# A four-layer graph network on one core: degrees counted by node tiles beside layer 0's messages, and inverse degrees found by a PE product inside layer 0

## The reference, cut to what matters

```python
x = layernorm(x + x @ W0)                  # W0: 256x256, edge weights scattered by (src, dst)
cnt = zeros((nodes, 4)).at[dst, etype].add(1.0)
inv_deg = 1.0 / maximum(cnt[dst, etype], 1.0)        # one number per edge
X = x
for l in range(4):
    h = einsum('ni,rio->rno', X, W[l])
    msg = h[etype, src] * inv_deg[:, None]
    agg = segment_sum(msg, dst)
    out = agg + X @ root[l] + bias[l]
    X = elu(layernorm(out) * gamma[l] + beta[l]) + X
out = layernorm(x + X)
```

## Time and profile before

| | |
|---|---|
| median of 3 runs | 2629.09 us (2626.32 to 2634.03) |
| the profiled execution's own time | 2628.71 us |
| its span | 2626.9 us |
| busy: PE, DVE, ACT, POOL | 82%, 55%, 11%, 59% |
| mean granted TensorE clock | 0.805 |

### The profile page before, as it was taken

How to read it: one execution, slowest core, us unless ns; L and a number is a source line. 1 busy time by engine, 2 the same in 40 slices (tenths; PEclk the granted TensorE clock), 3 DMA queues, 4 the chain that set the end, 5 groups by cost and what they waited for, 6 DMA issues and landing times.

```text
span 2626.9 us, 43114 instructions
## 1 busy us (share of the span) xinstructions
PE 2162.1 (82%) x7317; PEld 1284.5 (49%) x7320; DVE 1449.0 (55%) x4907; ACT 276.9 (11%) x538; POOL 1544.4 (59%) x1630
## 2 busy tenths in 40 slices
PE   4489667788888898888888989888889798887775
PEld 2254456664445554344455553445555444445554
DVE  6560999973445664234455652344556423456677
ACT  1114003310001111000011110000111100000000
POOL 3200600037777773777777737777777377777773
PEclk8589559996789998567889995678999956667778
DMA  5013300013444443334444433344444433334342
GB/s 165 0 41 144 130 8 0 0 42 106 120 129 138 145 149 96 105 105 121 129 136 146 145 104 104 106 120 129 138 145 147 140 110 104 105 104 121 105 121 64
DMA packets 103215, 280.43 MB, mean 107 GB/s; under 512 B 27676, under 2 KB 39050, under 8 KB 102798
## 3 DMA queue, kind: packets, MB, share of 16 engines
q0 software_dynamic: 75264, 205.62, 27.5%
q10 hardware_dynamic: 18224, 62.59, 6.2%
q1 hardware_dynamic: 9566, 10.42, 1.3%
HBM read 219.61 MB, written 58.91 MB: 106 GB/s over the span
## 4 chain that ended last, share of the span: by engine, by line
PE 50%; issue 13%; POOL 12%; DVE 9%; DMA 9%; DVEq 2%; POOLq 1%; ACT 1%; SPq 0%; ACTq 0%
PE acc L544 27%; POOL ring L335 12%; DMA ring<-h_rows,idx 8%; PE hp L463 8%; PE pw L463 7%; PE acc L533 3%; DVE S L993 3%; PE acc L536 2%; DVE hot_n L966 1%; DVE hot_s L966 1%; POOLq L204 1%; PE tr L452 1%; ACT XT L580 1%; DVEq L993 1%; PE pw L439 1%
## 5 line engine op out<-in xcount | busy, mean ns | idle before, releaser
L335 POOL DMA_INDIRECT ring<-h_rows,idx x1568 | 1506.3, 961 | 988.4 <-issue 715.2
L544 PE MATMUL acc<-ring,S 128*128 x3712 | 1247.8, 475 | 174.1 <-SPq L255 131.1
L1016 DVE TENSOR_SCALAR S<-iota,ecol 128x128 f32<-128x128 f32 x1856 | 611.7, 367 | 857.3 <-PE acc L544 753.8
L544 PEld LDWEIGHTS acc<-ring,S 128*128 128x128 f32 x3712 | 751.9, 224 | 662.0 <-issue 588.5
L463 PE MATMUL hp<-wts,XT 128*128 (+1 forms) x416 | 220.9, 681 | 22.4 <-ACT XT L580 22.4
L463 PE MATMUL pw<-wts,XT 128*128 (+1 forms) x384 | 197.9, 663 | 20.3 <-ACT XT L580 20.3
L533 PE MATMUL acc<-wts,XT 128*128 (+1 forms) x400 | 121.6, 432 | 62.3 <-issue 62.3
L966 DVE TENSOR_TENSOR hot_s<-iota,place 128x400 bf16<-128x400 f32 x196 | 111.5, 569 | 90.6 <-PE acc L494 85.8
L463 PEld LDWEIGHTS hp<-wts,XT 128*128 128x128 f32 x416 | 86.9, 220 | 126.2 <-issue 126.2
L533 PEld LDWEIGHTS acc<-wts,XT 128*128 128x128 f32 x400 | 81.0, 210 | 118.9 <-issue 110.0
L651 ACT ACTIVATE work<-work 128x256 f32<-128x256 f32 x100 | 41.7, 417 | 899.6 <-DVE work L1045 890.3
(11 more groups left out here) (243 smaller groups left out, 1085.6 us busy)
## 6 DMA issues: line engine op xcount, KB each, us to landing
h_rows<-hst ACTq DMA_DIRECT2D x100, 512.0 KB, 3.0
ring<-h_rows,idx POOLq DMA_INDIRECT x1568, 2.8
wts<-weights SPq DMA_DIRECT2D x32, 128.0 KB, 2.8
x_rows<-X ACTq DMA_DIRECT2D x1, 3200.0 KB, 10.0
wts<-x_rows ACTq DMA_DIRECT2D x1, 3200.0 KB, 11.5
X<-x SPq DMA_DIRECT2D x1, 3072.0 KB
out<-X ACTq DMA_DIRECT2D x2, 1024.0 KB
wts<-roots SPq DMA_DIRECT2D x8, 128.0 KB, 3.0
```

The lines of the kernel that those rows point to most:

```text
L335: pool.indirect_dma_start(ring[:, k, :], None, h_gather, bass.IndirectOffsetOnAxis(ap=idx[:, g * J + j:g * J + j + 1], axis=0)).then_inc(l ...
L544: nc.tensor.matmul(accs[t % 2][:, 0:D], S[:, at * J + j, :], ring[:, bass.ds((c + j) % SLOTS, 1), :].rearrange("p a d -> p (a d)"), start= ...
L1016: v.tensor_scalar(S[:, at * J + j, :], iota[:, t * P:(t + 1) * P], dst_c[:, bass.ds(c + j, 1)], inv_c[:, bass.ds(c + j, 1)], ALU.is_equal, ...
```

## The change

Stages 3 and 4 go. Instead:

- The edges' types become four rows of zeros and ones (ScalarE, from the natural order), go to DRAM and come back as `typ_rows`, in which the four types of the four columns of a group lie on 16 partitions, repeated three times and padded. They also become columns, `typ_hot`. `typ_rows` takes the place of the weights of layers 2 and 3, which are loaded after layer 0's last selection.
- Counting goes by node tiles. For each group of visits VectorE makes one 128x512 comparison of destinations with the tile's nodes (`add_hots`), TensorE multiplies each 128x128 part with four columns of `typ_hot` (`count`). It stands between the node products, five tiles behind them (LATE).
- The reciprocals are split into three bfloat16 parts, transposed to rows (25 transposes, four copies) and kept as `inv_rows`.
- In layer 0 the inverse degrees of a group are made by a product of `typ_rows` and `inv_sel` into the bank `rowb` (`select`, 512 columns), and `find` on VectorE reads it: it writes the four matrices of S and the inverse degrees, which are added to `inv_c` for the other layers. `inv_sel` is made once a tile (`selector`).
- Since `typ_rows` is addressed by groups, each tile's first column is rounded down to a multiple of four in the table, for all layers.

The diff, cut to its core:

```diff
@@ the table
+            col(v.tensor_scalar(coli[:, 0:1], c(19), 0.0, None, ALU.add))
+            col(v.tensor_scalar(coli[:, 1:2], coli[:, 0:1], J.bit_length() - 1, None, ALU.logical_shift_right))
+            col(v.tensor_scalar(c(19), coli[:, 1:2], float(J), None, ALU.mult))
             col(v.tensor_tensor(c(20), c(16), c(19), ALU.subtract))
@@ TensorE
-            pe.wait_ge(s["ld_w"], 16 * L * KH * (R + 1))
+            pe.wait_ge(s["ld_w"], 16 * (L // 2) * KH * (R + 1))
+            def count(t):
+                lo_t, end_t, w_t = tile_visits(pe, t)
+                with pe.Fori(lo_t, end_t, J) as c:
+                    pe.wait_ge(s["cnt_hot"], w_t + c + J)
+                    pe.sem_inc(s["passed"], 1)
+                    for j in range(J):
+                        nc.tensor.matmul(cnt_ps[:, t * R:(t + 1) * R], hot01[:, bass.ds((w_t + c) % (2 * J) + j, 1), :].rearrange("p a n -> p (a n)"),
+                                         typ_hot[:, bass.ds(c + j, 1), :].rearrange("p a r -> p (a r)"),
+                                         start=False, stop=True, skip_group_check=True).then_inc(s["cnt_mm"], 1)
...
             for t in range(NT):
                 if t + 1 < NT:
                     turn(t + 1, t + 1)
                 node_products(t, t, 0, t - 1 if t > 1 else None)
+                if t >= LATE:
+                    count(t - LATE)
+            for t in range(NT - LATE, NT):
+                count(t)
...
+            def select(t, c, v):
+                pe.wait_ge(s["sel_ready"], t + 1)
+                pe.wait_ge(s["S_ready"], v + 1)
+                pe.sem_inc(s["passed"], 1)
+                nc.tensor.matmul(rowb[:], typ_rows[:, bass.ds(c * ROW, P)], inv_sel[:, t % 2, :, :].rearrange("p j n -> p (j n)"),
+                                 start=True, stop=True).then_inc(s["t_sel"], J)
+            def first_layer():
+                pe.wait_ge(s["cnt_max"], 1)
+                visits = tile_visits(pe, 0)
+                gb_t = entry(pe, T_GB, 0, MAXV)
+                select(0, visits[0], visits[2] + visits[0])
+                for t in range(NT):
+                    lo_t, end_t, w_t = visits
+                    if t > 0:
+                        pe.wait_ge(s["y_ready"], t + (NT - 1))
+                    root_product(0, t)
+                    select(t, lo_t + J, w_t + lo_t + J)
+                    for i in range(2):
+                        four(t, lo_t + i * J, i, w_t + lo_t + i * J, gb_t + lo_t + i * J)
+                    with pe.Fori(lo_t + 2 * J, end_t, J) as c:
+                        select(t, c, w_t + c)
+                        four(t, c, 0, w_t + c, gb_t + c)
+                    if t + 1 < NT:
+                        visits = tile_visits(pe, t + 1)
+                        gb_t = entry(pe, T_GB + t + 1, 0, MAXV)
+                        select(t + 1, visits[0], visits[2] + visits[0])
+                    if t > 0:
+                        e = t + NT - 1
+                        turn(e, t - 1)
+                        node_products(e, t - 1, 1, e if t == 1 else e - 1)
@@ VectorE
+            def add_hots(t):
+                lo_t, end_t, w_t = tile_visits(dve, t)
+                with dve.Fori(lo_t, end_t, J) as c:
+                    dve.wait_ge(s["cnt_mm"], w_t + c + J)
+                    dve.sem_inc(s["passed"], 1)
+                    v.tensor_tensor(hot01[:, bass.ds((w_t + c) % (2 * J), J), :], iota[:, t * P:(t + 1) * P].unsqueeze(1).to_broadcast([P, J, P]),
+                                    dst_c[:, bass.ds(c, J)].unsqueeze(2).to_broadcast([P, J, P]), ALU.is_equal).then_inc(s["cnt_hot"], J)
...
+            def selector(t):
+                v.tensor_tensor(inv_sel[:, t % 2, :, :], inv_rows[:, t * P:(t + 1) * P].unsqueeze(1).to_broadcast([P, J, P]),
+                                quarter[:].unsqueeze(2).to_broadcast([P, J, P]), ALU.mult).then_inc(s["sel_ready"], 1)
+            def find(t, c, w, at, gated):
+                for j in range(J):
+                    if gated:
+                        dve.wait_ge(s["agg_mm"], w + (j + 1 + BIAS - J))
+                    if j == 0:
+                        dve.wait_ge(s["inv_add"], w + 1)
+                        dve.wait_ge(s["t_sel"], w + J)
+                        dve.sem_inc(s["passed"], 1)
+                    v.scalar_tensor_tensor(out=S[:, at * J + j, :], in0=iota[:, t * P:(t + 1) * P], scalar=dst_c[:, bass.ds(c + j, 1)],
+                                           in1=rowb[:, j * P:(j + 1) * P], op0=ALU.is_equal, op1=ALU.mult,
+                                           accum_out=found[:, bass.ds(w % (2 * J) + j, 1)]).then_inc(s["S_ready"], 1)
+                dve.wait_ge(s["S_ready"], w + (J + 1))
+                dve.wait_ge(s["inv_add"], w + (J + 1))
+                dve.sem_inc(s["passed"], 1)
+                v.tensor_tensor(inv_c[:, bass.ds(c, J)], inv_c[:, bass.ds(c, J)], found[:, bass.ds(w % (2 * J), J)], ALU.add).then_inc(s["inv_add"], J)
...
+            selector(0)
+            for t in range(NT):
+                lo_t, end_t, w_t = tile_visits(dve, t)
+                find(t, lo_t, w_t + lo_t, 0, True)
+                find(t, lo_t + J, w_t + lo_t + J, 1, False)
+                if t > 0:
+                    layer_norm_elu(0, t - 1, tile_end(t - 1), features(t - 1))
+                if t + 1 < NT:
+                    selector(t + 1)
+                with dve.Fori(lo_t + 2 * J, end_t, J) as c:
+                    find(t, c, w_t + c, 0, True)
@@ SyncE, behind layer 0's landings
+            sp.wait_ge(s["t_sel"], total)
+            for l in range(L // 2, L):
+                for k in range(KH):
+                    sp.dma_start(wts[:, l, k, 0:R * D].rearrange("p (r n) -> p r n", r=R),
+                                 weights[l, :, k * P:(k + 1) * P, :].rearrange("r p n -> p r n")).then_inc(s["ld_w2"], 16)
+                    sp.dma_start(wts[:, l, k, R * D:NB], roots[l, k * P:(k + 1) * P, :]).then_inc(s["ld_w2"], 16)
```

More of the change, by code:

```diff
@@ L29 @@
 BIAS = SLOTS + J
-HS = 32
-NH = NP // HS
 NB = 5 * D
-TB_COLS = 29
+TB_COLS = 32
 NC = NG * J
@@ L237, in _ @@
             sp.dma_start(X[0:N - (NT - 1) * P, NT - 1, :], x[(NT - 1) * P:N, :]).then_inc(s["ld_x"], 16)
-            for l in range(L):
+            for l in range(L // 2):
                 for k in range(KH):
@@ L484, in _ @@
                 node_products(t, t, 0, t - 1 if t > 1 else None)
-            pe.wait_ge(s["y_ready"], NT)
-            nc.tensor.matmul(cnt_ps, zeros[:, 0:NH], zeros[:, 0:P], start=True, stop=True)
-            with pe.Fori(0, NG // 2) as two:
-                for half in range(2):
-                    g = two * 2 + half
-                    pe.wait_ge(s["hot_ready"], g + 1)
-                    for j in range(J):
-                        m = nc.tensor.matmul(cnt_ps, hot_s[:, half, j, :], hot_n[:, half, j, :],
-                                             start=False, stop=True, skip_group_check=True)
-                    m.then_inc(s["cnt_mm"], 1)
@@ new lines, in _ @@
+            for t in range(NT - LATE, NT):
+                count(t)
+            parts_bank = rowb[:].bitcast(BF16)
+            pe.wait_ge(s["inv_split"], 5)
+            for u in range(-(-NT // 8)):
+                if u > 0:
+                    pe.wait_ge(s["inv_rows"], u)
+                for t in range(u * 8, min(u * 8 + 8, NT)):
+                    m = nc.tensor.transpose(parts_bank[:, (t - u * 8) * P:(t - u * 8 + 1) * P],
+                                            inv_parts[:, t, :, :].rearrange("p q k -> p (q k)"), ident_h[:])
+                m.then_inc(s["inv_tr"], 1)
@@ L553, in _ @@
             pe.wait_ge(s["ld_par"], 48)
-            with pe.Fori(0, L - 1) as l:
+            first_layer()
+            pe.wait_ge(s["ld_w2"], 16 * (L // 2) * KH * 2)
+            with pe.Fori(1, L - 1) as l:
                 lm = entry(pe, l + T_LM, 0, MAXV)
@@ L639, in _ @@
             act.dma_start(x1_rows, X[:].rearrange("p t d -> p (t d)")).then_inc(s["x1_saved"], 16)
-            with act.Fori(0, NG // 2) as two:
-                for half in range(2):
-                    g = two * 2 + half
-                    act.wait_ge(s["hot_tr"], g + 3)
-                    act.wait_ge(s["inv_mm"], g + 1)
-                    nc.scalar.activation(hot_t[:, half, :], (rowb, tr)[half][:].bitcast(BF16)[0:NH, 0:GE], ACT.Copy).then_inc(s["hot_t_ready"], 1)
+            parts_bank = rowb[:].bitcast(BF16)
+            for u in range(-(-NT // 8)):
+                act.wait_ge(s["inv_tr"], u + 1)
+                act.sem_inc(s["passed"], 1)
+                n = (min(u * 8 + 8, NT) - u * 8) * P
+                nc.scalar.activation(inv_rows[:, u * 8 * P:u * 8 * P + n], parts_bank[:, 0:n], ACT.Copy).then_inc(s["inv_rows"], 1)
             def elu_exp(el):
@@ L733, in _ @@
             columns(3, idx[:, 0:NG * J].rearrange("p (g j) -> p g j", j=J), rowb).then_inc(s["col_out"], 1)
-            dve.wait_ge(s["col_out"], 4)
-            for a in range(2):
```

(12 more changed lines are left out.)

269 lines of the change are left out of this document (142 added, 127 removed).

## The result

| | before | after |
|---|---|---|
| median, us (runs) | 2630.03 (4) | 2810.93 (4), 2807.83 to 2812.1 |
| ratio | 1 | 1.0686, 95% interval 1.0667 to 1.0704 |
| span of the profiled execution | 2626.9 | 2809.5 |
| granted clock, mean of the span | 0.805 | 0.790 |

The changed kernel is slower by 181 us. The spans differ by 182.6, and the stages say where that came from. Busy time by stage of the changed kernel, columns as in the earlier trace rows: products with the counts, inverse degrees, layer 0, layer 1.

A forecast was written before the change was run, and what follows sets the result against it. VectorE was taken to bound the counting and look-up stages, and gathers, thinly, layer 0. From 2628.7 us: minus 64 and 2 gained, plus 277 for layer 0 and 3 for later layers, gives 2842.7, said as 2842; range 2710 to 2940.

The forecast's parts named there:

- Counting, 303 us forecast: Counting moved beside layer 0's node products: products with counts and their uncovered last groups and loads take 303 us.
- The group of 1.7 us: One count group, a VectorE comparison and four small products with register addresses, takes 1.7 us; bounds 1.08 and 1.9.
- rival A: Count groups are paced by data, at 1.08 us each: 76 us less, 2766 us in all; chance 0.13.
- 64 and 2: Gains ahead of layer 0: 64 us by starting it earlier, 2 us at the start of the kernel.
- Layer 0, 764 forecast: With the look-up folded in, layer 0 takes 764 us against 487 before; bounds 641 and 870.
- I take 6.4 for them and a little for the rest: Layer 0's late tile: products at 6.4 us instead of 3.5 for a lower clock, making 22.6 us a tile.
- B: Clock stays at 2.4 GHz through layer 0: 641 us instead of 764, so 2720 in all; chance 0.12.
- E: Layer 0 runs at 1.2 GHz throughout: 870 us, so 2949 in all; chance 0.06.
- D: Order table doesn't grow to 492 visits, or table loads stay hidden: 40 to 50 us less; within the forecast's 0.62.
- The loads, 46 us: Table loads between a layer 0 tile's last visits and next selection cost 1.9 us a tile, 46 in all.
- The later layers, 3 forecast: Layers 1 to 3 get 28 more visits each from rounding: 1 us each, 3 together (0 to 12).
- Rival C: Layer 0's selection and norm chain stays under the gathers: layer 0 takes 525 us, total 2552; chance 0.07.

## Why the prediction was right, and where its terms were off

Predicted 2842 us (2710 to 2940), slower with 0.91; measured 2810.9. The mechanism was the one forecast, and it was shown twice: by the trace, and by the two runs that undo its parts. The distance of 31 us is a sum in which misses cancel: 8 too much was forecast as gained ahead of layer 0, layer 0 was put 44 too long, and the later layers 5 too short. The terms:

- **Counting, 303 us forecast, 312 measured; its tail 17 and 15.** The group of 1.7 us stood well (1.77 between two groups in the row above), and rival A fell: the fixed operands show that the addresses pace it. The loop that the 1.7 was taken from does not show it, though. In the earlier trace rows PE's idle time ends with a GpSimd operation, which waits for VectorE, which waits for PE (timeline of before):

```profile
60.44 0.21 DVE L855 TENSOR_TENSOR ring<-iota_b,ring 128x48 f32 x1 [0.57 <-PE tr L416]
61.13 0.71 POOL L314 TENSOR_TENSOR ring<-ring  x1 [0.81 <-DVE ring L855]
```

So its 1.5 us may have been the time of that ring of three engines, and that it was also near the price of the addresses is in part luck. What I missed is that a tile's third set of one-hots can only be built once its first group has been counted, which is behind the queued products. The run with the long ring prices that at 18 us. The gain was 58 where the sum had 64 and 2.

- **Layer 0, 764 forecast, 720 measured.** The chain of a late tile was right in its order and nearly in each link: select, turn and copy 1.17 (1.15 forecast), products 3.51 (1100.22 to the root at 1103.73; 3.5), four readers and the addition 1.6 (1.55), norm 4.7 (4.9). Visits and loads took 4.32, forecast as 4.3, but that match is luck: I had 2.1 of visits at 2.4 GHz and 2.2 of bare loads, and the row has 3.78 of visits at 1.2 GHz and 0.54 of idle time. With these links I had 19.45, and the turns show 19.4. The step that was mis-sized is "I take 6.4 for them and a little for the rest": the clock. I took the products as slow in each tile. They take 3.7 in some and 5.35 in others (1054.54), while the visits behind the wait are slow instead. The granted clock was 0.82, not the 0.7 I had carried over from the last layer. The nine tiles of three groups from 900 us on took 19.4 to 21.6 from turn to turn, 20.3 in the mean, against 22.6. A tile of four groups took 26.5 (turns at 1053.34 and 1079.86), as forecast (22.6 + 4.0), because there the loads and the slow pieces both show. Rivals B and E, one level of the clock throughout, did not come: 0.82. Neither did D: there are 492 visits, and the loads cost 51.
- **The loads, 46 us.** The run with the loads early measures 51.4, of which an estimated 36 are the loads and the rest goes with the clock, so the agreement is closer than the term was. By the Trainium skill (Advanced Engine Details and Errata, Engine Queue Depths) TensorE's queue is 64 deep, and loads would then be hidden. The trace disagrees as long as only four visits are queued in front: the wait for the last find holds the sequencer until they can run, and they cover 2 us at 2.4 GHz and 3.8 at 1.2. Ahead of the turn at 1079.86 the four loads run from 1076.7 to 1079.2, though the tile's last visits begin at 1075.28.
- **The later layers, 3 forecast (0 to 12), 8.0 measured.** I had the cause, not the size: I took it that further visits are nearly free where the gathers bound the layer. The last layer alone, where the earlier trace rows already had the lowest clock, has 4.6 of the 8: 535.3 us (2809.5 less 2274.20), against the 530.7 from its first gather at 2096.21 to the end of the span before.
- **Rival C**, the chain under the gathers, was excluded by the order on VectorE. The run with norm first and loads early shows how near it was: the same bank, the same products, and layer 0 in 543 us. But its late tiles still take 14.5 us, not under 11.5. So most of the price of folding the look-up into layer 0 was not the selection itself: of the 232 us that layer 0 lost, 175 lay in the place of the norm and of four loads, and some 57 stay.

Where those 57 us lie can be read from the turns of X in the run with norm first and loads early. The first six periods take 141.6 us (610.26 to 751.84), against 138.7 before. The other 18 take 280.2 (to 1032.09), against 226.3. In them TensorE waits 43.9 us for the matrices of VectorE and 1.1 for landed gathers; before it was 0.2 and 10.1. The last gather of layer 0 is issued at 958.43, 84 us before the first of layer 1. So the early tiles keep the pace of before, and the late ones follow the chain of selection and find, which is still longer than the gathers. Not settled: what in that chain costs most. VectorE's own table loads are a candidate, with 43.7 us of issue ahead of its finds in those 280, and no run moved them.

## What to carry to other kernels

When a wait is put into the middle of an engine's order, look at what is queued behind it that was overlapped before; here moving one call by a few lines was worth 108 us of 181. In a loop of small products, price the register instructions ahead of them; here taking nearly half of them away paid 12 us, because a short buffer was next in line. Count a buffer's depth across the work that stands between two of its uses, and before work is moved ahead of a store, ask which transfers wait for that store.

## What the runs showed of the hardware

- The clock changed within a tile. Before a wait of 4.77 us a visit took 0.45 us, behind it 0.95. With the waits shortened, PE's busy time for the same instructions in layer 0 fell from 490.8 to 414.0 us, and the granted clock rose from 0.82 to 0.98. Here an edit that removed a wait gave back more than the wait.
- On PE's sequencer a register instruction ahead of the count products took 42 to 121 ns, and their loop's branch mostly longer. All branches of line L518, the loop of the counts, in the changed kernel:

```profile
L518 PEldq COMPARE_BRANCH  x123: 76/208/227, 198.6 to 484.4; - x123
```

The Trainium skill has about 108 ns for a compare-and-branch (Advanced Engine Details and Errata, Control Flow Timing). Here it is about twice that, near 208, in the 98 cases in which the branch goes back, and 76 in the 25 in which a tile's loop ends. The groups outside the loop saved branches as well as addresses; the run with the fixed first groups does not tell the two apart.
